# A head's context multiplied by its reciprocals in four pieces instead of one

## The reference

```
qkv = xn @ attn_qkvw + attn_qkvb            # split into q, k, v of 32 heads of 32 features
scores = q @ k^T * 32**-0.5                 # per head 2048 x 2048
probs = softmax(scores)
ctx = probs @ v                             # per head 2048 x 32
x + (ctx @ attn_ow + attn_ob) + ffn(xn)
```

## Time and profile before

| | |
|---|---|
| time, median of 3 runs | 2847.87 us (2843.93 to 2850.26) |
| time of the profiled execution | 2850.67 us |
| its span | 2848.9 us |
| stages within the span | 0 to 750 inputs, 750 to 2575 attention, 2575 to 2849 output |
| busy in the span | PE 2751.8 (97%), PEld 1612.5, DVE 1637.0, ACT 1289.9, POOL 1733.5 us |
| mean granted TensorE clock | 0.978 |

### The profile page before, as it was taken

How to read it: one execution, slowest core, us unless ns; L and a number is a source line. 1 busy time by engine, 2 the same in 40 slices (tenths; PEclk the granted TensorE clock), 3 DMA queues, 4 the chain that set the end, 5 groups by cost and what they waited for, 6 DMA issues and landing times. The chain is left out here.

```text
span 2848.9 us, 36121 instructions
## 1 busy us (share of the span) xinstructions
PE 2751.8 (97%) x13776; PEld 1612.5 (57%) x13776; DVE 1637.0 (57%) x2553; ACT 1289.9 (45%) x2299; POOL 1733.5 (61%) x406
## 2 busy tenths in 40 slices
PE   7999999999799999999999999999999999997999
PEld 6888887778444444444444444444444444436887
DVE  8411111111778777777777778777877787724221
ACT  3111111110066666666666666666666666672100
POOL 0111111110199989898999899889989998982121
PEclk9999999999599999999999999999999999998999
DMA  4233333112611121112111211221122111004432
GB/s 140 98 129 112 110 110 111 66 66 89 162 27 38 38 60 34 38 38 60 35 41 35 60 35 42 45 50 38 38 51 44 38 38 35 9 16 144 128 103 92
DMA packets 145852, 188.56 MB, mean 66 GB/s; under 512 B 87152, under 2 KB 112240, under 8 KB 134896
## 3 DMA queue, kind: packets, MB, share of 16 engines
q1 hardware_dynamic: 145712, 186.70, 23.6%
HBM read 122.44 MB, written 63.69 MB: 65 GB/s over the span
## 5 line engine op out<-in xcount | busy, mean ns | idle before, releaser
L859 DVE TENSOR_REDUCE part_max<-ps_b 128x1 f32<-128x512 f32 x2048 | 1276.2, 682 | 399.8 <-PE ps_b L740 398.0
L706 POOL TENSOR_TENSOR psum_p<-psum_p,probs 128x2048 f32<-128x2048 f32 x316 | 1455.9, 4607 | 47.1 <-ACT probs L837 1.4
L837 ACT ACTIVATE probs<-ps_b 128x512 f32<-128x512 f32 x2048 | 1114.1, 597 | 743.7 <-PE ps_b L730 742.2
L730 PE MATMUL ps_b<-qp,kp 97*128 97x512 f32 x2048 | 880.4, 434 | 1.4 <-ACT probs L837 1.3
L740 PE MATMUL ps_b<-kp,qp 96*128 96x512 f32 x2048 | 765.7, 417 | 50.2 <-DVE part_max L859 35.6
L730 PEld LDWEIGHTS ps_b<-qp,kp 97*128 97x128 f32 x2048 | 386.3, 189 | 627.3 <-ACT probs L837 453.8
L758 PE MATMUL ps_b<-probs,vh 128*32 128x512 f32 x4096 | 556.5, 616 | 2.5
L740 PEld LDWEIGHTS ps_b<-kp,qp 96*128 96x128 f32 x2048 | 400.4, 196 | 146.7 <-DVE part_max L859 80.6
L232 POOL TENSOR_TENSOR wlo<-wraw,whi 128x1024 fp32r<-128x1024 f32 x29 | 69.5, 2397 | 612.7 <-ACT whi L335 612.7
L261 PE MATMUL ps_a<-xhi,whi 128*128 128x512 f32 (+1 forms) x928 | 370.7, 399 | 1.0 <-DVE elo L424 0.9
L261 PE MATMUL ps_a<-xlo,whi 128*128 128x512 f32 (+1 forms) x928 | 367.7, 396 | 0.0
(11 more groups left out here) (72 smaller groups left out, 1100.5 us busy)
## 6 DMA issues: line engine op xcount, KB each, us to landing
kp<-qk_scr SPq DMA_DIRECT2D x96, 256.0 KB, 4.1
qp<-qk_scr SPq DMA_DIRECT2D x96, 256.0 KB, 6.3
qk_scr<-ehi SPq DMA_DIRECT2D x16, 1024.0 KB, 3.9
qk_scr<-elo SPq DMA_DIRECT2D x16, 1024.0 KB, 6.7
wraw<-wcat SPq DMA_DIRECT2D x29, 512.5 KB, 7.5
craw<-cz_scr SPq DMA_DIRECT2D x16, 768.0 KB, 5.0
stage<-x SPq DMA_DIRECT2D x16, 512.0 KB, 4.4
v_scr<-elo SPq DMA_DIRECT2D x16, 512.0 KB, 3.3
```

The source lines that it names most:

```text
L706: pool.tensor_tensor(acc[:, :], (acc if n else probs[0])[:, :], probs[t % RING][:, :], ALU.add) \
L730: pe.matmul(ps[:, st_bank(g, j, b), :], kp[j][0:PACK + 1, t * P:(t + 1) * P], qp[j][0:PACK + 1, b * NQ:(b + 1) * NQ], start=True, stop=Tru ...
L837: act.activation(probs[t % RING][:, b * NQ:(b + 1) * NQ], ps[:, st_bank(g, j, b), :], ACT.Exp, scale=SCALE).then_inc(exp_done, 1)
L859: dve.tensor_reduce(part_max[jn % 2][:, tn, b:b + 1], ps[:, MAX_BANK + bank, :], AX_X, ALU.max) \
```

## The change

L889 is one instruction over 128 x 512 elements, behind the fourth maximum of step 10. The changed kernel makes four of it, over 128 columns each, one in each of the steps 10 to 13, behind the second maximum of that step. The waits for the context, the reciprocals and the free `out_ctx` stay ahead of the first piece. `ctx_ready` is raised by each piece, so that its readers wait for four times the count. SP's four stores wait for all four pieces as before. The last head's pieces follow each other at the end.

```diff
--- before.py
+++ after.py
@@ -654,7 +654,7 @@
 
             def store_ctx(g, j):
                 h = number(g, j)
-                sp.wait_ge(ctx_ready, h + 1)
+                sp.wait_ge(ctx_ready, QB * (h + 1))
                 for b in range(QB):
                     sp.dma_start(cz_scr[bass.ds(h * HD, HD), b * NQ:(b + 1) * NQ],
                                  out_ctx[j % 2][b * HD:(b + 1) * HD, :]).then_inc(ctx_stored[j % 2], 16)
@@ -814,7 +814,7 @@
             def take_raw(g, j):
                 h = number(g, j)
                 act.wait_ge(pv_done, 16 * (h + 1))
-                wait(act, ctx_ready, h - 1)
+                wait(act, ctx_ready, QB * (h - 1))
                 act.activation(raw_ctx[j % 2][:, :], ps[:, PV_BANK, :], ACT.Copy).then_inc(raw_done, 1)
 
             def take_sums(g, j):
@@ -873,20 +873,22 @@
                 wait(dve, recip_stored, 16 * h)
                 dve.reciprocal(recip_q[:, :], sums_q[:, :]).then_inc(recip_done, 1)
 
-            def normalise(g, j):
+            def normalise(g, j, part):
                 h = number(g, j)
-                dve.wait_ge(raw_done, h + 1)
-                if is_last(g, j):
-
-
-                    dve.wait_ge(sum_ready, h + 1)
-                    dve.wait_ge(ctx_ready, h)
-                    dve.reciprocal(recip_b[:, :], ps[:, SUM_BANK, :]).then_inc(recip_done, 1)
-                    dve.wait_ge(recip_done, h + 1)
-                else:
-                    dve.wait_ge(recip_loaded, 16 * QB * (h + 1))
-                wait(dve, ctx_stored[j % 2], 16 * QB * (2 * g + j // 2))
-                dve.tensor_tensor(out_ctx[j % 2][:, :], raw_ctx[j % 2][:, :], recip_b[:, :], ALU.mult) \
+                c = slice(part * P, (part + 1) * P)
+                if part == 0:
+                    dve.wait_ge(raw_done, h + 1)
+                    if is_last(g, j):
+
+
+                        dve.wait_ge(sum_ready, h + 1)
+                        dve.wait_ge(ctx_ready, QB * h)
+                        dve.reciprocal(recip_b[:, :], ps[:, SUM_BANK, :]).then_inc(recip_done, 1)
+                        dve.wait_ge(recip_done, h + 1)
+                    else:
+                        dve.wait_ge(recip_loaded, 16 * QB * (h + 1))
+                    wait(dve, ctx_stored[j % 2], 16 * QB * (2 * g + j // 2))
+                dve.tensor_tensor(out_ctx[j % 2][:, c], raw_ctx[j % 2][:, c], recip_b[:, c], ALU.mult) \
                     .then_inc(ctx_ready, 1)
 
             def row_maxima(g, j):
@@ -902,17 +904,18 @@
                     for b in range(QB):
                         if has_maxima(g, j, t):
                             take_max(g, j, t, b)
+                        if b == 1 and has_before and 0 <= t - NORMALISE_AT < QB:
+                            normalise(*head(g, j, -1), t - NORMALISE_AT)
                     if t == RECIPROCAL_AT and has_before:
                         reciprocal(*head(g, j, -1))
-                    if t == NORMALISE_AT and has_before:
-                        normalise(*head(g, j, -1))
                     if t == TRANSPOSED_AT - 1 and not last:
                         row_maxima(g, j)
                     if t == TRANSPOSED_AT and not last:
                         take_transposed(g, j)
 
             scheduled(dve, period)
-            normalise(*LAST)
+            for part in range(QB):
+                normalise(*LAST, part)
 
 
 def project_output(nc, x, w2, bias, cz_scr, w_early, early_loaded, out):
```

## The result

The changed kernel takes 3101.53 us (median of 4 runs, 3091.65 to 3102.65), the one before, measured beside it, 2847.32 us (2843.93 to 2850.26). The ratio is 1.0886, with a 95% interval of 1.086 to 1.0911: 254 us slower, 8.5 us for each of 30 heads.

The account below looks back on a forecast made before the run. TensorE was taken as the bound. Lateness +7.0 and clock +0.9 gave +7.9 us a head; 30 heads less 7 us gave +230, so 3078 us. The forecast's own range was 3018 to 3150, with case one 2930 to 3150.

Parts of the forecast that it names:

- its likeliest case: VectorE's four pieces each wait for a GpSimd addition's end, piece 0 missing its turn: 3078 us, chance 0.58.
- The first rival: Piece 0 gets the SBUF path in time, later pieces end one addition earlier: 3.4 us a head, 2950 us; chance 0.22.
- the 7 us taken off for three such heads: Where additions run later, piece 0 may get through: three heads guessed, half the chance, 4.5 us each.
- The third rival: Short pieces on VectorE do not wait for an addition's end and disappear in the gaps: 2779 us; chance 0.06.
- The fourth: TensorE's clock stays at 1.2 GHz from 1436 to beyond 1455: some 3.5 us a head more, 3180 us; chance 0.08.
- unit 1 of step 14 takes the blow: TensorE's unit needs the first bank reduced after piece 3: issued at 1450.75, late by 8.55 us a head.
- The tail of a piece and the spacing of the additions: A piece ends 0.2 us after GpSimd's addition; additions follow each other by 4.8 us.
- The clock: TensorE's low clock: one episode of 1.6 us in every head instead of 0.72, so +0.9 us a head.
- what the profile was to show: Pieces of 4.3, 2.4, 2.3, 2.2 us; PE's waits for maxima over 150 us, longest over 2; head 64 us.
- SP's stores and the load of the next maxima are hidden: Stores start at 1450.1, the load comes to 1451.9 and lands near 1454; hidden by 3 us.
- GpSimd ran dry: Named way to be wrong: GpSimd runs dry and leaves the path free before piece 3.

Follow-up runs that it names:

- e1: The changed kernel with each piece's second factor read from a PSUM score bank instead of recip_b, one maximum earlier: 2801.31 us, ratio 0.9825.
- e5: The changed kernel with GpSimd's additions 6 to 8 of a head's eleven cut into four of 512 columns: 2826.01 us, ratio 0.9926.
- e6: The kernel before with GpSimd's additions 6 to 8 of a head's eleven cut into four of 512 columns: 2786.79 us, ratio 0.979.
- e7: The changed kernel with two pieces of 256 columns, in steps 10 and 11, instead of four of 128: 2930.31 us, ratio 1.0285.
- e3: The changed kernel with all four pieces in one place, where the single instruction stood: 3034.65 us, ratio 1.0643.
- e2: The changed kernel with the reciprocals computed behind step 7 instead of 8: 2957.72 us, ratio 1.0372.
- e9: The changed kernel with reciprocals behind step 7, pieces in steps 9 to 12 and GpSimd's additions 5 to 7 cut: 2792.95 us, ratio 0.9821.
- e8: The changed kernel with transposed scores recomputed into their own bank in TensorE's waits of steps 11 and 14: 3062.65 us, ratio 1.0751.
- e10: The kernel before with the transposed scores of step 11, block 3, computed six times into the same bank: 2832.48 us, ratio 0.9958.
- e4: The kernel before with its single product moved behind the second maximum of step 11: 2785.86 us, ratio 0.977.

## Why the prediction was right, step by step

It gave 3078 us, 0.8% below the measured 3101.53, and its likeliest case is the one that came. The change moved by +254 us where +230 was forecast. Its timetable against the changed kernel's, on the clock of the trace of before (20.30 us earlier, which puts piece 0, at 1451.45, on 1431.15. Unit 1 of step 11, 1452.16 here and 1431.89 in the earlier trace rows, gives 20.27, so the start of piece 0 agrees within 0.03):

| | predicted | measured |
|---|---|---|
| piece 0 starts, ends | 1431.15, 1435.7 | 1431.15, 1435.59 |
| piece 1 ends | 1440.5 | 1440.28 |
| piece 2 ends | 1445.3 | 1445.00 |
| piece 3 ends | 1450.1 | 1449.67 |
| unit 1 of step 14 issued | 1450.75 | 1450.32 |
| its lateness | 8.55 | 8.15 |
| what the low clock costs a head | 1.6 | 2.5 |

The lateness is counted in the changed kernel's own rows: 1470.62 less (1452.16 + 3.96 + 3.10 + 3.10 + 0.15).

The cause: a product with both inputs in SBUF waits for the end of GpSimd's addition, whatever its size. e1 takes the second SBUF input away and the wait is gone; e5 and e6 shorten the addition and it shrinks; e7 halves the number of pieces and doubles their columns, and each piece lasts as before. Three independent edits, so this is shown. The Trainium skill's rule in "SBUF — State Buffer", "Who interferes with whom", that whoever comes first keeps the shared port for its whole instruction, agrees with these lengths. e3 adds something that the prediction did not have: between two additions there was room for two short products, not one.

The first rival, piece 0 early, did not happen in any of the 30 heads (piece 0 lasts 4.06 to 4.53 us in each), so the 7 us taken off for three such heads were wrong. Its mechanism is real, as e2 shows. That its price came close, 2950 where e2 measured 2957.72, is partly luck: the lateness is 3.4 us and not 4.05, and the low clock costs up to 2.6 us a head and not 1.6. The third rival, that a short piece does not wait for an addition, is refuted: in each head with maxima to take, the pieces of the change last 2.1 us and more. Where a piece has one input in PSUM (e1) it lasts 0.28 us, and where no addition runs the last head's four last 0.90 us together, at 2819.29. That is 0.2 more than the single product's 0.69, where the prediction reckoned with 0.7. The fourth did not happen: the clock came back in each head.

That unit 1 of step 14 takes the blow was right: the 1.89 us ahead of 1470.62 is the longest wait of the head, in e5 it is the only place where TensorE still waits for maxima, and in e9, with an earlier and shorter last piece, it does not wait there. That it is so because the transposed maxima take a fifth place in the ring of four banks is read from the order of the program; no run leaves them out.

The terms that were off. The tail of a piece and the spacing of the additions: GpSimd kept 4.7 us and not 4.8 with the short pieces between, so the lateness is 8.15, not 8.55: -12 us over 30 heads. The clock is the term that was mis-sized: I counted one episode of 1.6 us. It is low for some 6 us during and behind the last wait (the product at 1470.62 already lasts 0.79 us), and unit 2 follows unit 1 of step 14 by 5.28 us (1470.62 to 1475.90) instead of the 2.77 of the earlier trace rows: 2.5 us, +27 us; e8 gives 2.4 us in the heads where the fall is gone. The lateness and the clock missed in opposite directions, so the total is closer than the clock term alone would leave it. With measured terms: 8.15 - 1.54 + 2.5 - 0.72 = 8.39 us a head, 252 us, against 254; the two profiles show 64.87 - 56.31 = 8.56 us a head. With e10's 0.43 for the clock before, it would be 8.68 and 260 us; the price of the clock before is not settled better than between the two.

Of what the profile was to show: lengths 4.3, 2.4, 2.3, 2.2 against 4.44, 2.37, 2.40, 2.11; a head of 64 against 64.9. TensorE's waits for VectorE's reductions were to be over 150 us and are 143 (128.8 at L740 and 14.6 at the transposition), the longest at L740 1.9 and not over 2. That SP's stores and the load of the next maxima are hidden held:

```profile
...
1469.99 1.73 SPq L659 DMA_DIRECT2D cz_scr<-out_ctx  x4
1471.77 0.55 SPq L639 DMA_DIRECT2D qp<-neg_max  x1
...
```

The weight loads waited for those maxima once, 1.0 us. GpSimd ran dry (217.6 us for late tiles), but behind piece 3, not ahead of it.

## What to carry to other kernels

An instruction that must wait for another engine's instruction at a shared path pays for that wait by the instruction, not by the column. Cutting it into pieces and spreading them multiplies the wait. Cut the other engine's long instruction instead (e6, 2786.79 us), or leave one instruction and move it to where the wait falls in a gap (e4, 2785.86 us); the two are equally fast within the noise, and the fastest here. Count the wait as part of what you put into a gap: one product of 2.45 us behind a maximum of step 11 cost TensorE nothing, four pieces of 2.1 to 4.4 us in four gaps cost 254 us. And work out the margin by which an instruction makes or misses its turn (here 0.25 us at piece 0; without the miss the kernel is 144 us faster).

## What the runs showed of the hardware that was not expected

- Between two GpSimd additions that follow each other, two products of 128 columns passed (0.28 us each behind the wait), the second although the next addition's record had begun by then (e3: second piece from 1422.85, addition from 1422.92). Starts on GpSimd are rough in the profile, so which of the two read first there is not shown.
- A wait that lowers TensorE's clock costs more than itself. In e10 and e8, products that only compute the same bank again, put into the wait, made the kernel 13 and 39 us faster.
- The clock fell in every head of the change (longest wait 1.89 us) and in 13 of 30 heads of the kernel before (1.5 us at most). In e5, where the waits that are left last up to 1.1 us, the grant over the attention (834 to 2500) is 1.00, as in e4, which has none.
